# Layer 1's normalisations on GpSimd and ScalarE, a box sum and an output moved, and TensorE's passes written out

## The reference, cut to what matters

```python
def _gn(v, G=32, eps=1e-05):
    B_, C_, H_, W_ = v.shape
    g = v.reshape(B_, G, C_ // G, H_, W_)
    m = jnp.mean(g, axis=(2, 3, 4), keepdims=True)
    s = jnp.var(g, axis=(2, 3, 4), keepdims=True)
    return ((g - m) / jnp.sqrt(s + eps)).reshape(v.shape)

x = x + _L0_conv_ref(_gn(x), ...)
x = x + _L1_conv_ref(_gn(x), ...)
x = x + _L2_conv_ref(_gn(x), ...)
x = x + _L3_conv_ref(_gn(x), ...)
```

```python
s_sig = jax.nn.sigmoid(jnp.einsum('bc,bcn->bn', at.mean(-1), xc) / C2)[:, None, :]
spatial_map = (s_sig * xc).reshape(Bv, C2, Hv, Wv)
c_sig = jax.nn.sigmoid(jnp.einsum('bcn,bn->bc', at, xc.mean(1)) / N)[:, :, None]
channel_map = (c_sig * at).reshape(Bv, C2, Hv, Wv)
out = jnp.concatenate([spatial_map, channel_map], axis=1)
return _pw(out, proj_out_w, proj_out_b)
```

## Time and profile before

| what | value |
|---|---|
| median of 3 runs | 1662.26 us (1662.19 to 1664.59) |
| the profiled execution's own time | 1665.31 us |
| its span, from first to last instruction | 1663.5 us |
| TensorE busy | 1542.7 us, 93% of the span |
| VectorE busy | 1097.4 us, 66% |
| ScalarE busy | 686.3 us, 41% |
| GpSimd busy | 50.2 us, 3% |
| mean granted TensorE clock | 0.974 of full speed |
| one pass, from first offset product to first offset product | 196 to 197 us |

### The profile page before, as it was taken

One profiled execution on the slowest core, in us unless ns is written; L12 is line 12 of the kernel. 1 busy time (PEld: TensorE's weight loads), 2 busy tenths in 40 slices (PEclk: granted clock), 3 DMA queues, 4 the chain that ended last, 5 costly groups with the idle time before them and its releaser, 6 DMA issues.

```text
span 1663.5 us, 22283 instructions
## 1 busy us (share of the span) xinstructions
PE 1542.7 (93%) x7252; PEld 827.6 (50%) x7252; DVE 1097.4 (66%) x2107; ACT 686.3 (41%) x1098; POOL 50.2 (3%) x76
## 2 busy tenths in 40 slices
PE   2879999899999999999998999989999899999975
PEld 1537553565436554365534754355543655337421
DVE  4358449864698457984489745985569845797266
ACT  2126325462345514454254622555145541456132
POOL 2000000000000000000000000000000000000000
PEclk9989999999999999999999999999999999999977
DMA  3000000100001000100001000010000100000000
GB/s 121 2 26 2 7 1 1 52 4 6 1 1 53 7 2 1 52 3 8 1 0 52 2 7 1 1 52 7 3 1 13 40 7 2 1 26 2 0 0 25
DMA packets 7964, 24.56 MB, mean 15 GB/s; under 512 B 1664, under 2 KB 2368, under 8 KB 7792
## 3 DMA queue, kind: packets, MB, share of 16 engines
q1 hardware_dynamic: 7792, 22.40, 3.8%
HBM read 12.13 MB, written 8.39 MB: 12 GB/s over the span
## 4 chain that ended last, share of the span: by engine, by line
PE 74%; DVE 13%; issue 6%; ACT 5%; POOL 1%; SPq 0%; DVEq 0%; DMA 0%; POOLq 0%; ACTq 0%
PE psO L523 15%; PE psN L523 15%; PE psN L861 11%; PE psO L727 8%; PE psN L727 5%; PE psN L634 5%; PE psO L583 4%; ACT samp L945 3%; DVE samp L1732 2%; PE psN L565 2%; PE psN L571 2%; PE psN L601 2%; DVE pool_v L1426 1%; PE psM L507 1%; DVE hf L1539 1%
## 5 line engine op out<-in xcount | busy, mean ns | idle before, releaser
L523 PE MATMUL psN<-xn,w 128*128 128x512 f32 x576 | 277.1, 604 | 0.9 <-DVE yout L1446 0.9
L523 PE MATMUL psO<-samp,w 128*128 128x512 f32 x576 | 270.1, 603 | 0.0
L634 PE MATMUL psN<-GQt,xq 64*128 64x144 f32 x1536 | 135.4, 313 | 27.0 <-issue 20.5
L1157 ACT ACTIVATE samp<-psN,vec 128x512 f32<-128x512 f32 x160 | 110.0, 687 | 116.3 <-PE psN L861 116.3
L945 ACT ACTIVATE samp<-psN 128x576 f32<-128x576 f32 x192 | 119.2, 685 | 86.3 <-PE psN L634 85.1
L523 PEld LDWEIGHTS psO<-samp,w 128*128 128x128 f32 x576 | 101.2, 190 | 95.3 <-issue 88.8
L1353 DVE COPY xblk<-psN 120x256 f32<-120x256 f32 x128 | 54.3, 424 | 129.9 <-PE psN L565 129.8
L523 PEld LDWEIGHTS psN<-xn,w 128*128 128x128 f32 x576 | 98.8, 189 | 81.7 <-issue 81.5
L945 ACT ACTIVATE G<-psN 120x256 f32<-120x256 f32 x128 | 49.1, 383 | 216.2 <-PE psN L571 216.2
L634 PEld LDWEIGHTS psN<-GQt,xq 64*128 64x128 f32 x1536 | 115.8, 200 | 41.2 <-issue 31.8
L727 PE MATMUL psN<-img,w 128*128 128x512 f32 x288 | 133.4, 608 | 0.0
(11 more groups left out here) (157 smaller groups left out, 2232.9 us busy)
## 6 DMA issues: line engine op xcount, KB each, us to landing
xin<-in_x SPq DMA_DIRECT2D x16, 512.0 KB, 4.4
out<-yout SPq DMA_DIRECT2D x16, 512.0 KB, 2.6
pool_v<-rows SPq DMA_DIRECT2D x72, 25.5 KB
w<-in_w SPq DMA_DIRECT2D x2, 576.0 KB, 5.7
samp<-in_r SPq DMA_DIRECT2D x1, 576.0 KB, 7.2
tab<-in_tab SPq DMA_DIRECT2D x1, 513.0 KB, 5.3
kh_w<-in_kh SPq DMA_DIRECT2D x1, 320.0 KB, 5.7
kv_w<-in_kv SPq DMA_DIRECT2D x1, 320.0 KB, 5.9
```

The costliest lines, as they stand in the source:

```text
L523: last = mm(dst[:, h, :], wgt[:, k, :], rhs(h, k), start=(k == 0), stop=(k == K9 - 1))
L634: last = mm(pair(s, u)[:, g, :].rearrange("p (k r c) -> p k r c", k=K9, c=SW)[:, :, :, cols], xQ[rows, t, a, e, :], w[rows, e, :, :, cols] ...
L1157: nc.scalar.activation(out, bank(m)[0:out.shape[0]], fn, **kw).then_inc(l3_act.sem, 1)
```

## The change

- `affine` on GpSimd takes the place of `affine_var` and `affine_scale` on VectorE, for L1A and L1B alone: ScalarE copies the two means out of PSUM (`means`), and GpSimd does seven operations on 128 x 1 elements: a square, a difference, the addition of EPS, the power, a multiplication by 1/9, one by -1, and their product. Each waits for the one before, save that the two multiplications behind the power go together. ScalarE does `normalise` for L1A ahead of the gate's sigmoids, and for L1B ahead of the strips.
- VectorE's first two parts of image 0's box sum stand around the gated map, in its wait for the gate. ScalarE scales `wo2`.
- `store_ready` of image 1 goes from the end of `second_half` into the next `first_half`, behind image 1's whole box sum and the first offsets, in the place of the box sum's last part. TensorE's first two blocks go to other PSUM banks, and its waits on `y_ready` stand where the banks are taken.
- TensorE's loop is written out: 8 copies of both halves.

```diff
 def block_bank(s, n):
-    return (psT[:, n % 2, :], psO0[:, n % 2, :])[n // 2 % 2 if s == 0 else 0]
+    return (psT[:, n % 2, :], psO0[:, n % 2, :])[(n // 2 + 1) % 2 if s == 0 else 0]
...
+            def affine(j, i, name, order):
+
+                g, k = norm(name), SAMPLE[name]
+
+                pool.wait_ge(means_ready.sem, means_ready.at(j, k + 1))
+                nc.gpsimd.tensor_tensor(out=g[:, 16:17], in0=g[:, 14:15], in1=g[:, 14:15], op=ALU.mult).then_inc(pool_own.sem, 1)
+                pool.wait_ge(pool_own.sem, pool_own.at(j, 2 * k + 1))
+                nc.gpsimd.tensor_tensor(out=g[:, 16:17], in0=g[:, 15:16], in1=g[:, 16:17], op=ALU.subtract)\
+                    .then_inc(pool_own.sem, 1)
+                pool.wait_ge(pool_own.sem, pool_own.at(j, 2 * k + 2))
+                nc.gpsimd.tensor_tensor(out=g[:, 17:18], in0=g[:, 16:17], in1=consts[:, 0:1], op=ALU.add)\
+                    .then_inc(var_ready.sem, 1)
+                rsqrt(i, name, order)
+                pool.wait_ge(rstd_ready.sem, rstd_ready.at(i, nth(name, order)))
+                nc.gpsimd.tensor_tensor(out=g[:, 19:20], in0=g[:, 18:19], in1=consts[:, 1:2], op=ALU.mult)\
+                    .then_inc(scale_ready.sem, 1)
+                nc.gpsimd.tensor_tensor(out=g[:, 16:17], in0=g[:, 14:15], in1=consts[:, 2:3], op=ALU.mult)\
+                    .then_inc(scale_ready.sem, 1)
+                pool.wait_ge(scale_ready.sem, scale_ready.at(j, 2 * k + 2))
+                nc.gpsimd.tensor_tensor(out=g[:, 20:21], in0=g[:, 16:17], in1=g[:, 19:20], op=ALU.mult)\
+                    .then_inc(affine_ready.sem, 1)
...
                 offset_parts(2, img[0], w1off)
                 offsets(i, 2, 27)
-
-                pe.wait_ge(y_ready.sem, y_ready.at(i, 0))
                 blocks(i, 0, range(2))
                 doubles(i, 0)
+                pe.wait_ge(y_ready.sem, y_ready.at(i, -1))
                 pe.wait_ge(pooled_ready.sem, pooled_ready.at(i, 2))
                 offset_parts(3, img[1], w1off)
                 far(i, 2)
+                pe.wait_ge(y_ready.sem, y_ready.at(i, 0))
                 blocks(i, 0, range(2, TILES))
                 offsets(i, 3, 27)
...
-            first_half(0)
-            with pe.Fori(0, PASSES - 1) as i:
-                second_half(i, True)
-                first_half(i + 1)
-            second_half(PASSES - 1, False)
+            for i in range(PASSES):
+                first_half(i)
+                second_half(i, i < PASSES - 1)
...
+            def means(j, i, name, order):
+
+                act.wait_ge(group_ready.sem, group_ready.at(i, nth(name, order)))
+                copy(norm(name)[:, 14:16], ps[SAMPLE[name]][:, 0:2]).then_inc(means_ready.sem, 1)
...
                     sums(i + 1, i, "L1A", order)
+                    means(i + 1, i, "L1A", order)
+                    normalise(i, "L1A", order)
                 for h in range(2):
                     maps(P_GATE + h, sg[:, HALF * h:HALF * h + HALF], ACT.Sigmoid)
...
+                nc.scalar.activation(wo2, woT[:, :, 1, :], ACT.Copy, scale=st3[:, 2:3]).then_inc(l3_scaled.sem, 1)
                 if more:
-                    normalise(i, "L1A", order)
                     sums(i + 1, i, "L1B", order)
+                    means(i + 1, i, "L1B", order)
+                    normalise(i, "L1B", order)
                     strips(i + 1, 0)
-                    normalise(i, "L1B", order)
...
                 def between(s):
-                    if s == 0:
-                        pool3(own, 1, 3, i, FIRST)
+                    if s == 0 and store:
+                        store_ready(i - 1, 1)
                     double(s)
-                for part in range(3):
+                for part in range(4):
                     pool3(own, 1, part, i, FIRST)
```

More of the change, by code:

```diff
@@ L453, in _ @@
             nc.gpsimd.memset(neg_half[:], -0.5).then_inc(borders_zero, 1)
-            pool.wait_ge(borders_zero, 8)
+            for n, value in enumerate((EPS, 1.0 / 9, -1.0)):
+                nc.gpsimd.memset(consts[:, n:n + 1], value).then_inc(borders_zero, 1)
+            pool.wait_ge(borders_zero, 11)
             def rsqrt(i, name, order):
@@ L461, in rsqrt @@
                                         op=ALU.pow).then_inc(rstd_ready.sem, 1)
+            def affine(j, i, name, order):
[17 more added lines that the diff above has]
+                    .then_inc(affine_ready.sem, 1)
             def one_pass(i, more):
                 for name in EVENTS if more else LAST:
-                    rsqrt(i, name, EVENTS if more else LAST)
+                    if name in ("L1A", "L1B"):
+                        affine(i + 1, i, name, EVENTS)
+                    else:
+                        rsqrt(i, name, EVENTS if more else LAST)
             for name in FIRST:
-                rsqrt(0, name, FIRST)
+                if name in ("L1A", "L1B"):
+                    affine(0, 0, name, FIRST)
+                else:
+                    rsqrt(0, name, FIRST)
             if PASSES > 1:
@@ L1518, in layer0, with store_ready, first_half @@
                     dve.sem_inc(GT_ready.sem, 2 * TILES)
-            def first_half(i, more):
+            def store_ready(i, s):
+                dve.wait_ge(l3_product.sem, l3_product.at(i, P_OUT + s))
+                v_.scalar_tensor_tensor(yout[s][:], final[s].rearrange("p b c -> p (b c)"),
+                                        vec[:, V_BOUT:V_BOUT + 1], yout[s][:], ALU.add, ALU.add)\
+                    .then_inc(y_ready.sem, 1)
+            def first_half(i, more, store=True):
                 own = Own(dve, dve_own, i)
@@ L1784, in second_half @@
                 v_.tensor_scalar(wss, blk64, st3[:, 4:5], 1.0 / N, ALU.mult, ALU.mult).then_inc(l3_wss.sem, 1)
-                if more:
-                    affine_var(own, "L1A", order)
                 dve.wait_ge(l3_act.sem, l3_act.at(i, P_MEAN + 1))
@@ L1793, in second_half @@
                 if more:
-                    affine_scale(own, "L1A", order)
+                    pool3(own, 0, 0, i, order)
                 dve.wait_ge(l3_act.sem, l3_act.at(i, P_GATE + 1))
                 v_.tensor_tensor(sm, sg, xc[:], ALU.mult).then_inc(l3_maps.sem, 1)
-                dve.wait_ge(l3_csig.sem, l3_csig.at(i, 1))
-                v_.tensor_scalar(wo2, woT[:, :, 1, :], st3[:, 2:3], None, ALU.mult).then_inc(l3_maps.sem, 1)
-                def store_ready(s):
-                    dve.wait_ge(l3_product.sem, l3_product.at(i, P_OUT + s))
-                    v_.scalar_tensor_tensor(yout[s][:], final[s].rearrange("p b c -> p (b c)"),
-                                            vec[:, V_BOUT:V_BOUT + 1], yout[s][:], ALU.add, ALU.add)\
-                        .then_inc(y_ready.sem, 1)
                 if more:
-                    pool3(own, 0, 0, i, order)
+                    pool3(own, 0, 1, i, order)
                     residual0(i + 1, 1)
-                    for part in range(1, 4):
+                    for part in range(2, 4):
                         pool3(own, 0, part, i, order)
-                    affine_var(own, "L1B", order)
-                store_ready(0)
-                if more:
-                    affine_scale(own, "L1B", order)
-                store_ready(1)
-                if more:
+                store_ready(i, 0)
+                if not more:
+                    store_ready(i, 1)
+                else:
                     assert own.n == DVE_STEPS, own.n
@@ L1843, in _ @@
             for s in range(2):
-                affine(first, ("L1A", "L1B")[s], FIRST)
                 for part in range(0 if s else 4):
```

21 lines of the change are left out of this document (15 added, 6 removed).

## The result

| | before | changed |
|---|---|---|
| median, 9 runs each | 1662.26 us | 1652.68 us |
| range | 1658.21 to 1666.76 | 1649.52 to 1656.55 |
| profiled execution, its span | 1665.3, 1663.5 us | 1652.05, 1650.3 us |
| TensorE busy | 93% | 93% |

The ratio is 0.9944, with an interval of 0.9928 to 0.996: 9.3 us faster, and 4 us slower than the 1648.8 that I forecast.

The account below looks back on a forecast made before the run. TensorE, busy for 93% of the span, was taken as the bound, its waits being all there is to win. 1665.3 - 25.2 (stalls) + 10.2 (later tables) - 1.5 (start) = 1648.8 us, range 1639 to 1669.

Parts of the forecast that it names:

- The stalls: Before `near`, TensorE's six stalls at the loop's branch back go when the passes are written out: 25.2 us less.
- The rival that the stall isn't the loop's: The stall before `near` stays or comes elsewhere, and only the start is won: 1664 us, chance 0.10.
- A delay of the tables would have been hidden by the stall: Before the change, nearly 3 us of delay in VectorE's tables for `near` would have been hidden by the loop's stall.
- GpSimd's price: Each new GpSimd multiplication or sum in the normalisations takes 0.20 us, bounds 0.09 and 0.55.
- the cheap rival: GpSimd's operations take 0.09 us and are not held, so no residual moves: 1637 us, chance 0.15.
- the slow one: GpSimd's seven operations each cost what the power does and become the bound: 1675 us, chance 0.17.
- GpSimd held: In image 0's normalisation GpSimd stands while VectorE reads two SBUF tensors; the scale is ready at 685.9.
- The group mean of image 1: Image 0's late normalisation delays residual 1, so TensorE's group mean moves from 693.65 to 694.65: +1.0 us.
- 1.45 a turn on the path: VectorE's tables for `near` start 1.45 us later, from 0.2 and the output addition's 1.27: 7 x 1.45 = +10.2 us.
- The wait of 1.9 before `offsets`: TensorE waits 1.9 us for ScalarE's offset parts, at no further cost while VectorE's box parts end later.
- the rival of the falling clock: The clock falls in the wait before `offsets`, +1.7 us in each of 7 turns: 1661 us, chance 0.16.
- The start and the end: Ahead of pass 0, nothing to 2.9 us less, taken as 1.5; at the kernel's end, at most 0.3 us.

Follow-up runs that it names:

- e1: The kernel before with only TensorE's loop changed, written out: 1638.18 us, ratio 0.9835 to the kernel before.
- e3: e1 with two passes in each turn of TensorE's loop, so that it goes back twice: 1645.43 us, ratio 0.9885.
- e2: The changed kernel with TensorE's loop put back: 1673.68 us, ratio 1.0052 to the kernel before.
- e9: e7 with image 1's normalisation given back to VectorE, image 0's part and the changed start kept: 1637.36 us, ratio 0.9833.
- e12: The changed kernel with 6 idle products on TensorE between the offset products and `offsets`: 1651.30 us, ratio 0.9926.
- e7: e6 with the box sum's last part also put back between the first offsets and the tables: 1641.14 us, ratio 0.9852.
- e6: The changed kernel with strips ahead of image 1's normalisation and the output's addition back at the end of `second_half`: 1650.96 us, ratio 0.9925.
- e8: e1 with image 1's normalisation alone given to GpSimd and ScalarE, strips behind it: 1649.30 us, ratio 0.9913.
- e4: The changed kernel with ScalarE's strips ahead of image 1's normalisation again: 1650.11 us, ratio 0.9907.

## Why the prediction was right or wrong

**The stalls: right, a little smaller.** 25.2 us in the sum; 23.2 by the profiles of before and e1, and e3 ties them to the branch back. The sum took pass 7's 18.99 us as what a pass takes without a stall, but the inner passes of e1 take 19.41 to 19.51 for the same stretch. The 27.3 of e1's median hold 3.8 us from the start and the end of the kernel, which the sum didn't have. The rival that the stall isn't the loop's falls.

**A delay of the tables would have been hidden by the stall: wrong.** e2 should then have been near 1661, and took 1673.7. There TensorE itself comes later, by its two waits and the slower clock, and the stall is in series with that.

**GpSimd's price: right.** 0.20 taken, 0.19 measured, so the cheap rival's 0.09 and the slow one's 0.55 both fall: alone image 1's chain takes 2.0 us (689.52 to 691.55), where I had 2.3.

**GpSimd held: right in sum, wrong in how.** The scale of image 0 is ready 4.9 us behind the end of its group mean (675.44 to 680.33), as I had (681.0 to 685.9). But I gave it a turn between two operations of VectorE. Instead its first product stood for 1.82 us, while three of them ended back to back, and ended only when VectorE had paused for 0.04 us (677.49 to 677.53). The second stood for 0.64 under the next one, and the rest had more room than I gave them.

**The group mean of image 1: right** (1.0 in the sum; its wait is 0.91). As a cost it was wrong: e9 has it and loses nothing, since the box sum is done before the mean, and the wait that stood behind the mean goes.

**1.45 a turn on the path: right in size, wrong in what it was made of.** The sum has the tables 11.85 us behind the mean (706.5 less 694.65), and with the clock kept they are 11.77 behind it (e12). Against the 192.85 of e1, the turns in which the clock stays at 1.00 up to `near` are 192.67 with image 0's part (e9), 193.17 with image 1's on GpSimd too (e7), 194.13 with the last box part ahead of the offsets' tables (e6), 194.44 with the addition and the strips in their new places (e12, with the six products in the wait): +1.6 in all. The steps that failed are "the addition stands between the first offsets and the tables", priced at 1.27, and "the box sum's last part only changes sides of the offsets", priced at nothing. It is nearly the other way round: 0.3 for addition and strips together, 0.96 for the part. The addition stands mostly where VectorE waits for L644 anyway. Of this ladder the part (e6, e7) and image 1's scale (e9, e7) were each tried in one pair; e12 differs from e6 in three things, and its 0.3 is their sum. That the single costs come near the forecast's 1.45 is largely luck.

**The wait of 1.9 before `offsets` "costs nothing further": wrong, and without it the forecast would not have been too low.** The wait is there (1.59) and the clock falls behind it. A turn of the changed kernel is 195.24 on average instead of e12's 194.44. The tables show it pass by pass: they start 12.23, 12.24, 12.46, 12.71, 13.72, 12.28 and 12.33 us behind the mean, where e12 has 11.77 with the clock kept. The excess is 0.5 to 2.0 us a pass, 5.6 over the seven. This is the rival of the falling clock, with half of its price: it counted 1.7 in each turn. How much it costs goes by how early behind the wait the clock falls. At 1085 us it is in `offsets` already, which take 3.07 instead of 1.97.

**The start and the end: more than the sum had.** `near` of pass 0 begins at 128.69 before and 125.77 in the changed kernel, 2.9 earlier, where I took 1.5. Other kernels with the old start have it at 127.3 to 129.1, those with the new one and no added products at 125.4 to 126.5: 2.1 on average. Behind `near` of pass 7 the changed kernel takes 158.6 us and before took 162.1, where the sum had nothing; that stretch differs by as much between kernels that share its code, and no run says why.

**How the sum closes.** From `near` of pass 0 to that of pass 7 the changed kernel takes 1365.9 us where e1 takes 1349.5. Of these 16.4 the clock is 5.6, and 10.8 are the path's, for which the sum had 10.2. Against the sum, on the profiled executions: 2.0 less won by the stalls, 5.6 lost by the clock, 0.6 more on the path, and on the other side 1.4 more at the start and 3.5 at the end. That is 3.3 us; measured, 1652.05 less 1648.8, 3.2. So errors of 8 and of 5 us stand against each other, and that the forecast came within 4 us is in part luck.

Forecast of `near` waiting 1 to 1.6 us for the table: 1.00 in e12, where the clock is kept, and 0 to 0.63 in the changed kernel, as TensorE itself comes later behind the slower clock.

**Open.** The price of the clock rests on turns of the profiles of the changed kernel, e8 and e12; e12 as a whole is only 1.4 us under the changed kernel by the medians and 3 by the ratios, and the intervals overlap; its products cost 1.6 us in pass 0, where they fill no such wait. The two experiments with twelve products overshot. Why the clock falls in some turns and not in others behind the same wait was not found; in e12 it fell once with the wait filled, and in two passes of e4 it stayed at 1.00 up to `near` behind a wait of 1.8. That GpSimd is held through a run of VectorE's is read from the timelines; no kernel was made for it. e1 and e9 can't be told apart; with 1638.2 and 1637.4 us they are the fastest versions found, 1.1% under the changed kernel by the ratios.

## What to carry to other kernels

Cost a branch back as a stall in series: it is added to whatever makes the engine late, and longer turns pay it less often (twice instead of six times in e3). An operation that seems to be in the way on the critical engine may only fill a wait; ask where the answer it waits for comes from, and keep useful work between the request and the answer (the box part between the first offsets and the tables) before moving anything else. A new wait on TensorE of 1.6 us is priced with the clock behind it, and not as idle time alone; the clock's fall costs where TensorE's answer is what the next engine waits for (the offsets here), and hardly where VectorE's tables set the pace (`near` in e1).

## What the runs showed of the hardware

- TensorE's loop over some 195 us of work cost 2.6 to 3.1 us of standstill at each branch back. With the slower clock behind it a turn was 3.0 to 4.6 us longer than in e1, 3.8 on average, and 3.4 in e3. In e2, where TensorE itself comes later, it still cost 3.3.
- A GpSimd product of 128 x 1 takes 0.19 us from start to end, a power 0.55. Beside VectorE operations that read two SBUF tensors it was held until VectorE paused: 1.82 for one, 0.69 for another under the 1.22 us sum. The power that began at 678.61, just ahead of that sum, wasn't. This is the sharing of SBUF interfaces that the Trainium skill names (GPSIMD Engine Reference, § 1 Specifications), and the trace agrees; that it lasts through several operations is this trace's own.
- Behind the 1.59 us wait the granted clock fell in all seven passes of the changed kernel, to 0.50 in two of the three shown. Behind the 1.27 us of e1 it stayed at 1.00 up to `near`, and all turns were alike. With 1.01 (e8) it fell in three of seven passes: 0.56 in 891 to 893 us of e8.
- A product of 72 columns took 0.23 us (12 in 2.74), not in proportion to the 0.12 or so that I had taken for it.
